# The reciprocal root of the variances on VectorE by Newton steps instead of a square root on ScalarE, in a gated cross-attention and mixture-of-experts kernel

## The chip, the cores and the metric

One core of one Trainium2 chip runs the whole program. The metric is the device time of one execution in microseconds. The kernel before took 3248.48 us, the median of 3 runs (3244.9 to 3255.8).

## The reference

For each of 8 batches of 512 rows of 512 numbers:

```
x  = x + tanh(g0) * attention(layernorm(x), ctx)      # 16 heads of 32, 1601 context rows, q and o quantised to int8 steps
x  = x + tanh(g1) * (experts(h) + shared(h)), h = layernorm(x)
layernorm(x) = (x - mean) / sqrt(var + 1e-5)          # over the 512 numbers of a row
quantise(x): s = max|x| / 127 ; clip(round(x / s), -127, 127) * s
```

The experts part picks 4 of 32 experts for each of the 4096 rows (sigmoid scores, best 2 of 4 groups), each of capacity 128, and a shared gated network runs beside it. The variances of the two layer norms are what the change touches: 4 numbers on each of 128 partitions per batch and norm.

## The kernel before

**Attention part.** The work goes batch by batch (b, 8), in each batch by groups of 4 heads (g, 4), and in each group by 13 tiles of 128 context rows (kt, "key tile"; the last has 65 rows). One step (b, g, kt) is, for each of the 4 heads: a score matmul into one of two PSUM tiles (`scores_of`, L810), its exponential on ScalarE into `probs` (L1038), the matmuls with the values (`heads_of`, L824, one step later), and for 10 of the 13 key tiles (all but 4, 8 and 12) an add of `probs` to `prob_acc` on GpSimd (`add_probs`, L1510; a copy, L1507, for the first tile). The score matmul of a head waits until the exponential two heads earlier has emptied its PSUM tile. `probs` has three buffers in turn.

**Fill work.** Between the score matmuls of a step stand tiles of other work, in an order that is written out by hand (`lead_tiles`, `fill_tiles`) and is the same on TensorE, ScalarE and VectorE: every engine goes through its own instructions in that order, so a wait of one instruction holds all that stand behind it on its engine. For the next group these are the queries, the keys in four pieces (two at kt 0, two at kt 1; ScalarE rounds them, L996, VectorE makes the rest, `k_lo`, L1246), and from kt 3 to 11 the row maxima: 32 pairs of matmuls (L732) into two banks each, read by one VectorE reduction (L1253). There are four such banks, so two pairs can be under way. The keys and queries of a head are stacked by DMAs on SyncE's queue before its first maxima. In group 2 the context tiles of the next batch come in as well (transposes L682, `ctx_hi` on ScalarE L986, `ctx_lo` on VectorE L1218): tiles 0 and 1 at kt 2, tiles 2 and 3 at kt 3, and so on; their DMAs are issued behind those of the keys.

**The two norms.** Their steps stand behind the fill work of a step. For the next batch's x they are in group 2 (`x_part`): at kt 1 the statistics (VectorE, bn_stats and bn_aggr, `variances`), at kt 2 the square root (ScalarE, `deviations`, L929), at kt 3 reciprocal and shift (VectorE, `inverse_std`, L1170 and L1172), at kt 4 and 5 the normalising (ScalarE, L935), then scale, round, clip and integers up to kt 11. For the last batch's h they are in group 1 (`h_part`): statistics at kt 0, square root at kt 1, reciprocal at kt 2, normalising at kt 3 and 4. For batch 0 the x steps stand among the first context tiles, before the attention loop; for the last batch the h steps stand in the experts part, between the first shared tiles, and the rows of the second block are read back from DRAM behind them. Exponential and square root need different tables on ScalarE: a load stands before the first of each (ACT_TABLE_LOAD).

**Experts part.** From about 2530 us: per block of 512 rows the shared network and the routing on VectorE, then the 32 experts with indirect DMAs on GpSimd.

Of the kernel before, what the change touches and what calls it, by code (L numbers as in the profile page):

```python
# [26 lines left out]
P = 128  # L27
# [15 lines left out]
EPS = 1e-5  # L43
ROUND = 12582912.0
CT_SLOTS = 3
SBANKS, NBANKS, HALVES = 2, 4, 3
# [5 lines left out]
CTX_AT = [2, 2, 3, 3, 4, 5, 6, 7, 8, 9, 10, 11, 12]  # L52
X_STATS, X_STD, X_RSTD, X_NORM, X_SCALE, X_ROUND, X_CLIP, X_INT = 1, 2, 3, (4, 5), 6, (7, 8), (8, 9), (10, 11)
O_SCALE, O_ROUND, O_CLIP, O_INT, O_TURN, Y_AT = 3, (4, 5), (5, 6), (7, 8), 9, 10
H_STATS, H_STD, H_RSTD, H_NORM, LATE_HEADS = 0, 1, 2, (3, 4), 10
HALF_TILES = (range(TT // 2), range(TT // 2, TT))
# [180 lines left out]
def build(nc, x, ctx_in, g_xattn, g_ffn, wq, bq, wkv, bkv, wp, bp, gate_w, gate_bias, w1, w2, w3,  # L237
# [15 lines left out]
    with ctx:  # L253
# [12 lines left out]
        lane = sb("lane", [P, E], FP32)  # L266
        eps = sb("eps", [P, 1], FP32)
        rounder = sb("rounder", [P, 2], FP32)
# [21 lines left out]
        mv = sb("mv", [P, TT, 2], FP32)  # L290
        std = sb("std", [P, TT], FP32)
        rstd = sb("rstd", [P, TT], FP32)
# [111 lines left out]
        ctx_raw_in = [sem(f"ctx_raw_in{i}") for i in range(CT_SLOTS)]  # L404
        x_var_ready = sem("x_var_ready")
        x_std_ready = sem("x_std_ready")
        h_var_ready = sem("h_var_ready")
        h_std_ready = sem("h_std_ready")
        x_rstd_ready = sem("x_rstd_ready")
# [500 lines left out]
        def _(act):  # L910
# [14 lines left out]

            def deviations(ready, count, done):

                act.wait_ge(ready, count)
                nc.scalar.activation(std[:, :], mv[:, :, 1], ACT.Sqrt, bias=eps[:, :]).then_inc(done, 1)  # L929

            def normalised(dst, tiles, ready, count, done):
# [19 lines left out]
            def x_part(b, at):  # L951

                if at == X_STD:
                    deviations(x_var_ready, b + 1, x_std_ready)
                for half, tiles in enumerate(HALF_TILES):
                    if at == X_NORM[half]:
                        normalised(xin, tiles, x_rstd_ready, b + 1, x_normed)
                    if at == X_ROUND[half]:
                        rounded(xin, tiles, x_inv_ready, b + 1, x_rounded)
                    if at == X_INT[half]:  # L960
                        integers(xin, tiles, x_clipped, b * TT, x_quantised)
# [9 lines left out]
            def h_part(b, at):  # L971

                if at == H_STD:
                    deviations(h_var_ready, b + 1, h_std_ready)
                for half, tiles in enumerate(HALF_TILES):
                    if at == H_NORM[half]:
                        normalised(work, tiles, h_rstd_ready, b + 1, h_ready)
# [101 lines left out]
            for f in range(B):  # L1079
                for key in ffn_tiles(f):  # L1080
                    tile(key)
                    if key == ("y", B - 1, TT - 1):
                        for at in (H_STD,) + H_NORM:
                            h_part(B - 1, at)
# [15 lines left out]
        def _(dve):  # L1100
# [55 lines left out]

            def variances(ready):
                for t in range(TT):
                    step.mark(V.bn_stats(stats[:, t, :], xin[:, t, :]))
                step.settle()  # L1160
                for t in range(TT):
                    last = V.bn_aggr(mv[:, t, :], stats[:, t, :])
                    if t < TT - 1:
                        step.mark(last)
                last.then_inc(ready, 1)

            def inverse_std(done, n, ready):

                dve.wait_ge(done, n)
                step.mark(V.reciprocal(rstd[:, :], std[:, :]))  # L1170
                step.settle()
                V.scalar_tensor_tensor(out=shift[:, :], in0=mv[:, :, 0], scalar=-1.0, in1=rstd[:, :],  # L1172
                                       op0=ALU.mult, op1=ALU.mult).then_inc(ready, 1)
# [7 lines left out]
            def x_part(b, at):  # L1181

                if at == X_STATS:
                    dve.wait_ge(x_in, (b + 1) * DMA)
                    variances(x_var_ready)
                elif at == X_RSTD:
                    inverse_std(x_std_ready, b + 1, x_rstd_ready)
                elif at == X_SCALE:
                    dve.wait_ge(x_normed, (b + 1) * TT)
                    row_scales(xin, sx)  # L1190
                    dve.sem_inc(x_inv_ready, 1)
                elif at in X_CLIP:
                    clip_rows(xin, HALF_TILES[X_CLIP.index(at)], x_rounded, b * TT, x_clipped)
# [9 lines left out]
            def h_part(b, at):  # L1203

                if at == H_STATS:
                    step.settle()
                    variances(h_var_ready)
                elif at == H_RSTD:
                    inverse_std(h_std_ready, b + 1, h_rstd_ready)

# [260 lines left out]
        def _(pool):  # L1471
            step = Steps(pool, pool_step, pool_wait_carrier)
            G = nc.gpsimd
            for m in (ident, identb):
                step.mark(G.memset(m[:, :], 0.0))
            for m, v in ((onesb, 1.0), (ones, 1.0), (tri, 1.0), (eps, EPS), (zero_rows, 0.0), (slot_init, 0.0)):
                ap = m[:, :, :] if m is slot_init else m[:, :]
# [130 lines left out]
```

## Time and profile before

| | |
|---|---|
| time, median of 3 runs | 3248.48 us (3244.9 to 3255.8) |
| profiled execution | 3254.07 us, span 3251.4 us |
| TensorE matmul busy | 2811.8 us, 86% |
| GpSimd busy | 1806.8 us, 56% |
| VectorE busy | 1727.0 us, 53% |
| ScalarE busy | 1387.3 us, 43% |
| granted TensorE clock, mean | 0.95 |

The span is from the first to the last instruction of the profiled execution, and all times in the rows below count from its start. "Busy" counts instructions that compute. In a row of the timeline a bracket says how long the engine had been idle before the instruction and what ended it. The granted clock is a share of TensorE's full 2.4 GHz; 0.5 is 1.2 GHz.

### The profile page before, as it was taken

Reading aid. Unit: us, or ns where it says so; the run is one execution under the profiler, and the core shown is the slowest. Engines: PE = TensorE matmul, PEld = TensorE weight load, DVE = VectorE, ACT = ScalarE, POOL = GpSimd, SP = SyncE. Lnnn points to the kernel's source line nnn. Section 1 sums busy time; section 2 is a strip of 40 time slices with the busy share of each in tenths; the row PEclk is TensorE's granted clock in tenths of the full one; section 3 lists DMA queues with packets and bytes.
Section 4 is the critical chain, followed back from the end, with each engine's and each line's share of the span. In section 5 each row is a group of like instructions: output and inputs, shape, how many; then the busy total and the mean of one; then the engine's idle time right before and its main releaser. Section 6 shows DMA issues by size and latency. Waiting matters only on the chain. (4 is left out here: it accounts for less than half of the span.)

```text
span 3251.4 us, 42577 instructions
## 1 busy us (share of the span) xinstructions
PE 2811.8 (86%) x14876; PEld 1192.9 (37%) x14876; DVE 1727.0 (53%) x2854; ACT 1387.3 (43%) x2460; POOL 1806.8 (56%) x1570
## 2 busy tenths in 40 slices
PE   5898988899889888988899898889888689996986
PEld 3223333333333333333333333333332344443765
DVE  6566556656565656566556655665653324342222
ACT  3155445644564455455545544564456211010111
POOL 0285566556655665657566656755669223324555
PEclk9799999899999999999999999999999789998999
DMA  4111012110211031103112101211011221222997
GB/s 127 33 44 52 21 34 70 52 35 20 78 48 44 11 97 39 34 21 92 29 34 69 52 21 34 69 52 34 21 51 29 79 89 66 78 78 73 271 279 194
DMA packets 146578, 215.53 MB, mean 66 GB/s; under 512 B 24984, under 2 KB 78232, under 8 KB 146368
## 3 DMA queue, kind: packets, MB, share of 16 engines
q1 hardware_dynamic: 130496, 195.95, 20.0%
q0 software_dynamic: 15872, 16.87, 2.8%
q8 instruction: 120, 1.97, 0.3%
q14 instruction: 90, 0.74, 0.1%
HBM read 126.49 MB, written 34.24 MB: 49 GB/s over the span
## 5 line engine op out<-in xcount | busy, mean ns | idle before, releaser
L1510 POOL TENSOR_TENSOR prob_acc<-prob_acc,probs 128x512 f32<-128x512 f32 x1152 | 1430.1, 1275 | 484.7 <-ACT probs L1038 484.2
L1038 ACT ACTIVATE probs<-s_ps 128x512 f32<-128x512 f32 (+1 forms) x1664 | 939.0, 596 | 806.8 <-PE s_ps L810 787.3
L1253 DVE TENSOR_REDUCE piece_max<-r_all 128x2 f32<-128x802 f32 (+1 forms) x1024 | 965.2, 986 | 229.1 <-PE r_all L732 223.6
L810 PE MATMUL s_ps<-q_stack,k_flat 97*128 97x512 f16 (+1 forms) x1664 | 630.0, 397 | 73.9 <-ACT probs L1038 66.0
L732 PE MATMUL r_all<-k_flat,q_stack 96*128 96x401 f16 (+1 forms) x2048 | 552.3, 353 | 131.7 <-DVE piece_max L1253 80.2
L824 PE MATMUL o_ps<-probs,v_sb 128*32 128x512 f32 (+1 forms) x3328 | 462.8, 629 | 21.4 <-ACT probs L1038 21.4
L810 PEld LDWEIGHTS s_ps<-q_stack,k_flat 97*128 97x128 f16 (+1 forms) x1664 | 161.5, 102 | 635.6 <-ACT probs L1038 411.5
L1507 POOL COPY prob_acc<-probs 128x512 f32<-128x512 f32 x128 | 72.8, 612 | 507.2 <-PE sum_ps L844 372.2
L732 PEld LDWEIGHTS r_all<-k_flat,q_stack 96*128 96x128 f16 x2048 | 178.3, 100 | 392.7 <-DVE piece_max L1253 143.1
L1542 POOL DMA_INDIRECT slot_rows<-payload,slot x128 | 125.3, 979 | 317.7 <-DVE slot L1440 194.7
L1246 DVE SCALAR_TENSOR_TENSOR k_lo<-r_all,bk_col,k_hi 128x400 f16<-128x400 f32 (+1 forms) x128 | 81.8, 639 | 280.7 <-ACT k_hi L996 280.7
L779 PE MATMUL r_all<-probs,k_flat 128*128 128x512 f32 x512 | 225.9, 603 | 2.0 <-DMA k_flat<-in_L_ffn_shared_down 2.0
L1225 DVE TENSOR_TENSOR v_sb<-r_all,bv_row 128x512 f32<-128x512 f32 (+1 forms) x104 | 71.8, 691 | 195.3 <-PE r_all L692 195.2
L996 ACT ACTIVATE k_hi<-r_all,bk_col 128x400 f16<-128x400 f32 (+1 forms) x128 | 76.5, 598 | 197.5 <-PE r_all L721 197.5
L1568 POOL DMA_INDIRECT out_rows<-probs,slot_init x64 | 99.7, 1559 | 96.1 <-DMA out_rows<-probs,slot_init 50.0
L779 PEld LDWEIGHTS r_all<-probs,k_flat 128*128 128x128 f32 x512 | 98.5, 194 | 123.1 <-issue 121.0
L692 PE MATMUL r_all<-wkv_hi,ctx_hi 128*128 128x512 f16 (+1 forms) x416 | 113.1, 396 | 21.0 <-DVE piece_max L1253 18.5
L824 PEld LDWEIGHTS o_ps<-probs,v_sb 128*32 128x32 f32 (+1 forms) x3328 | 66.7, 109 | 159.6 <-issue 88.0
L797 PE MATMUL r_all<-k_flat,probs 128*128 128x512 f32 x256 | 119.6, 628 | 0.9 <-DVE probs L1396 0.9
L1218 DVE TENSOR_TENSOR ctx_lo<-r_all,ctx_hi 128x512 f16<-128x512 f32 (+1 forms) x104 | 69.2, 673 | 76.0 <-ACT ctx_hi L986 75.6
L721 PE MATMUL r_all<-ctx_hi,wkv_hi 128*128 128x400 f16 (+1 forms) x512 | 109.4, 336 | 0.0
L721 PE MATMUL r_all<-ctx_lo,wkv_hi 128*128 128x400 f16 (+1 forms) x512 | 109.1, 336 | 0.0
(193 smaller groups left out, 2752.8 us busy)
## 6 DMA issues: line engine op xcount, KB each, us to landing
k_flat<-k_hi SPq DMA_DIRECT2D x256, 100.1 KB, 2.2
ctx_raw<-in_ctx SPq DMA_DIRECT2D x96, 256.0 KB, 2.9
v_sb<-in_L_ffn_w SPq DMA_DIRECT2D x48, 512.0 KB
xin<-in_x SPq DMA_DIRECT2D x16, 1024.0 KB, 5.6
k_flat<-k_lo SPq DMA_DIRECT2D x128, 100.1 KB, 2.2
ctx_hi<-in_L_ffn_w SPq DMA_DIRECT2D x24, 512.0 KB
ctx_lo<-in_L_ffn_w SPq DMA_DIRECT2D x24, 512.0 KB
q_stack<-q_hi SPq DMA_DIRECT2D x256, 32.0 KB, 1.8
```

The lines of the kernel that those rows point to most:

```text
L692: last = nc.tensor.matmul(ps[0:w, :], a[:, c, t * P:t * P + w], wt[:, 1, c, :], start=(n == 0), stop=(n == 3 * DC - 1))
L721: last = nc.tensor.matmul(ps[:, 0:w], wt[:, 0, c, g * P:(g + 1) * P], a[:, c, at:at + w], start=(n == 0), stop=(n == 3 * DC - 1))
L732: last = nc.tensor.matmul(ps[:, 0:w], q_stack[0:KSPLIT, g % 2, j, qt * P:(qt + 1) * P], k_stack[0:KSPLIT, g % 2, j, at:at + w], start=True ...
L779: last = nc.tensor.matmul(ps[:, :], wt[:, c, f * P:(f + 1) * P], hT[:, c, :], start=(c == 0), stop=(c == DC - 1))
L797: last = nc.tensor.matmul(ps[:, :], actT[:, f, t * P:(t + 1) * P], sd[:, f, :], start=(f == 0), stop=(f == FSC - 1))
L810: nc.tensor.matmul(s_ps[j % SBANKS][0:w, :], k_stack[:, g % 2, j, kt * P:kt * P + w], q_stack[:, g % 2, j, :], start=True, stop=True).then ...
L824: last = nc.tensor.matmul(o_ps[j * DH:(j + 1) * DH, :], v_sb[0:w, kt, h * DH:(h + 1) * DH], probs[0:w, slot, j, :], start=(kt == 0), stop= ...
L1038: nc.scalar.activation(probs[0:w, slot, j, :], s_ps[j % SBANKS][0:w, :], ACT.Exp).then_inc(probs_ready, 1)
L1253: V.reduce_max(piece_max[:, j * TT + qt, 2 * i:2 * i + 2], r_all[:, k:k + 2, 0:MAX_WIDE[i]], X_AXIS).then_inc(free_of(*key), 1)
L1510: last = G.tensor_tensor(prob_acc[:, j, :], prob_acc[:, j, :], probs[:, slot, j, :], ALU.add)
L1542: G.indirect_dma_start(out=slot_scr, out_offset=bass.IndirectOffsetOnAxis(ap=slot[:, t, k:k + 1], axis=0), in_=payload[:, t, k, :], in_off ...
L1568: G.indirect_dma_start(out=out, out_offset=bass.IndirectOffsetOnAxis(ap=e_slots[:, e, 0:1].bitcast(I32), axis=0), in_=e_y[e % 2][:, h * HA ...
```

## The change

The square root on ScalarE and its semaphores go. VectorE now makes 1 / sqrt(var + eps) by itself: it adds eps, takes a first guess from the bits of the number (a shift to the right, times -1, plus a constant), and betters it by three Newton steps of three instructions each, every one waiting for the one before. All later steps of x and h move one key tile forward, since one step of the sequence is gone.

```
-X_STATS, X_STD, X_RSTD, X_NORM, X_SCALE, X_ROUND, X_CLIP, X_INT = 1, 2, 3, (4, 5), 6, (7, 8), (8, 9), (10, 11)
+X_STATS, X_RSTD, X_NORM, X_SCALE, X_ROUND, X_CLIP, X_INT = 1, 2, (3, 4), 5, (6, 7), (7, 8), (9, 10)
-H_STATS, H_STD, H_RSTD, H_NORM, LATE_HEADS = 0, 1, 2, (3, 4), 10
+H_STATS, H_RSTD, H_NORM, LATE_HEADS = 0, 1, (2, 3), 10
...
-            def deviations(ready, count, done):
-                act.wait_ge(ready, count)
-                nc.scalar.activation(std[:, :], mv[:, :, 1], ACT.Sqrt, bias=eps[:, :]).then_inc(done, 1)
...
-            def inverse_std(done, n, ready):
-                dve.wait_ge(done, n)
-                step.mark(V.reciprocal(rstd[:, :], std[:, :]))
-                step.settle()
+            def inverse_std(ready):
+                step.mark(V.tensor_scalar(var[:, :], mv[:, :, 1], EPS, None, ALU.add))
+                step.settle()
+                step.mark(V.tensor_scalar(shift[:, :].bitcast(I32), var[:, :].bitcast(I32), 1, None, ALU.logical_shift_right))
+                step.settle()
+                step.mark(V.tensor_scalar(rstd[:, :].bitcast(I32), shift[:, :].bitcast(I32), -1.0, RSQRT_SEED, ALU.mult, ALU.add))
+                step.settle()
+                for _ in range(NEWTON):
+                    step.mark(V.scalar_tensor_tensor(out=shift[:, :], in0=rstd[:, :], scalar=-0.5, in1=rstd[:, :],
+                                                     op0=ALU.mult, op1=ALU.mult))
+                    step.settle()
+                    step.mark(V.tensor_tensor(shift[:, :], shift[:, :], var[:, :], ALU.mult))
+                    step.settle()
+                    step.mark(V.scalar_tensor_tensor(out=rstd[:, :], in0=shift[:, :], scalar=1.5, in1=rstd[:, :],
+                                                     op0=ALU.add, op1=ALU.mult))
+                    step.settle()
                 V.scalar_tensor_tensor(out=shift[:, :], in0=mv[:, :, 0], scalar=-1.0, in1=rstd[:, :],
                                        op0=ALU.mult, op1=ALU.mult).then_inc(ready, 1)
```

`NEWTON` is 3. `variances` now ends with a wait for its own last bn_aggr, in place of a signal to ScalarE, and the memset of the constant `eps` on GpSimd is gone.

## Rows read from the trace of the kernel before

**Rows 1.** Groups of instructions on ScalarE: busy us, mean ns, idle before.

```profile
L929 ACT ACT_TABLE_LOAD x16 | 20.5, 1283 | 0.3
L1038 ACT ACT_TABLE_LOAD x15 | 19.2, 1283 | 0.3
```

**Rows 2.** Timeline at an h site (batch 1, group 1): start, duration, instruction.

```profile
512.18 4.95 POOL L1510 TENSOR_TENSOR prob_acc<-prob_acc,probs 128x512 f32<-128x512 f32 x4
...
516.51 1.28 ACT L929 ACT_TABLE_LOAD   x1
516.53 0.64 DVE L1246 SCALAR_TENSOR_TENSOR k_lo<-r_all,bk_col,k_hi 128x400 f16<-128x400 f32 x1 [2.93 <-ACT k_hi L996]
...
519.42 3.32 ACT L1038 ACTIVATE probs<-s_ps 128x512 f32<-128x512 f32 x6
520.07 0.88 PE L810 MATMUL s_ps<-q_stack,k_flat 97*128 97x512 f16 x2 [2.78 <-ACT probs L1038]
...
521.86 0.67 PE L732 MATMUL r_all<-k_flat,q_stack 96*128 96x401 f16 x2
...
524.33 0.61 PE L810 MATMUL s_ps<-q_stack,k_flat 97*128 97x512 f16 x1
```

**Rows 3.** Timeline at the same place of batch 0, where no statistics stand.

```profile
203.61 12.29 POOL L1510 TENSOR_TENSOR prob_acc<-prob_acc,probs 128x512 f32<-128x512 f32 x10
...
207.96 0.64 DVE L1246 SCALAR_TENSOR_TENSOR k_lo<-r_all,bk_col,k_hi 128x400 f16<-128x400 f32 x1 [2.93 <-ACT k_hi L996]
...
212.05 0.85 PE L732 MATMUL r_all<-k_flat,q_stack 96*128 96x401 f16 x2 [1.44 <-DMA k_flat<-k_hi]
```

**Rows 4.** Timeline of dependent small VectorE instructions, with no GpSimd add beside them.

```profile
2583.01 0.17 DVE L1375 TENSOR_SCALAR wsum<-wsum 128x4 f32<-128x4 f32 x1
2583.21 0.18 DVE L1377 RECIPROCAL wrec<-wsum 128x4 f32<-128x4 f32 x1
```

**Rows 5.** Durations ns (min/median/max) of two lines, and timelines where VectorE meets GpSimd.

```profile
L1108 DVE TENSOR_SCALAR so<-amax x8: 169/1306/1322, 444.1 to 2539.7; 128x4 f32<-128x4 f32 x8
...
444.07 1.30 DVE L1108 TENSOR_SCALAR so<-amax 128x4 f32<-128x4 f32 x1
444.09 3.70 POOL L1517 TENSOR_TENSOR xin<-xin,bp_row 128x512 f32<-128x512 f32 x3
...
L1510 POOL TENSOR_TENSOR prob_acc<-prob_acc,probs x1152: 1250/1267/1732, 141.1 to 2530.2; 128x512 f32<-128x512 f32 x192
...
491.34 0.69 DVE L1268 TENSOR_TENSOR xin<-xin,work 128x512 f32<-128x512 f32 x1
491.43 1.73 POOL L1510 TENSOR_TENSOR prob_acc<-prob_acc,probs 128x512 f32<-128x512 f32 x1 [1.75 <-ACT probs L1038]
```

**Rows 6.** Timeline at an x site (batch 0, group 2).

```profile
267.25 8.63 POOL L1510 TENSOR_TENSOR prob_acc<-prob_acc,probs 128x512 f32<-128x512 f32 x7
...
274.80 1.28 ACT L929 ACT_TABLE_LOAD   x1
...
275.30 0.38 PE L810 MATMUL s_ps<-q_stack,k_flat 97*128 97x512 f16 x1
...
276.10 1.88 DVE L1253 TENSOR_REDUCE piece_max<-r_all 128x2 f32<-128x802 f32 x2
...
281.58 0.66 PE L682 MATMUL r_all<-ident,ctx_raw 128*128 128x128 f32 x4 [1.84 <-DMA ctx_raw<-in_ctx]
```

**Rows 7.** Timeline at the first exponentials.

```profile
138.58 0.88 PE L810 MATMUL s_ps<-q_stack,k_flat 97*128 97x512 f16 x2 [2.17 <-ACT probs L1038]
```

**Rows 8.** Timeline at the last h, in the experts part.

```profile
2593.46 0.30 ACT L929 ACTIVATE std<-mv,eps 128x4 f32<-128x4 f32 x1 [8.71 <-DVE mv L1162]
...
2594.20 2.93 ACT L935 ACTIVATE work<-xin,shift,rstd 128x512 f32<-128x512 f32 x4 [0.44 <-DVE shift L1172]
...
2608.09 3.38 PE L766 MATMUL r_all<-ident,probs 128*128 128x128 f32 x16 [20.43 <-DMA probs<-h_rows]
```

**Rows 9.** Busy time by stretch: us, each engine's, granted clock, DMA share, GB/s.

```profile
522.30:525.60 3.30, 3.30 (x13) 0.77 (x13) 0.99 (x1) 1.00 (x2) 3.30 (x4) 0.52 0.69 162
```

More of the change, by code:

```diff
@@ L44 @@
 ROUND = 12582912.0
+RSQRT_SEED, NEWTON = 1597463007.0, 3
 CT_SLOTS = 3
@@ L266, in build @@
         lane = sb("lane", [P, E], FP32)
-        eps = sb("eps", [P, 1], FP32)
         rounder = sb("rounder", [P, 2], FP32)
@@ L290, in build @@
         mv = sb("mv", [P, TT, 2], FP32)
-        std = sb("std", [P, TT], FP32)
+        var = sb("var", [P, TT], FP32)
         rstd = sb("rstd", [P, TT], FP32)
@@ L404, in build @@
         ctx_raw_in = [sem(f"ctx_raw_in{i}") for i in range(CT_SLOTS)]
[L405 to L408, printed above, removed]
         x_rstd_ready = sem("x_rstd_ready")
@@ L951, in x_part @@
             def x_part(b, at):
-                if at == X_STD:
-                    deviations(x_var_ready, b + 1, x_std_ready)
                 for half, tiles in enumerate(HALF_TILES):
@@ L971, in h_part @@
             def h_part(b, at):
-                if at == H_STD:
-                    deviations(h_var_ready, b + 1, h_std_ready)
                 for half, tiles in enumerate(HALF_TILES):
@@ L1082, in _ @@
                     if key == ("y", B - 1, TT - 1):
-                        for at in (H_STD,) + H_NORM:
+                        for at in H_NORM:
                             h_part(B - 1, at)
@@ L1155, in _, with variances @@
             V.tensor_scalar(bp_row[:, :], bp_row[:, :], tanhs[:, 0:1], None, ALU.mult).then_inc(row_consts_ready, 1)
-            def variances(ready):
+            def variances():
                 for t in range(TT):
@@ L1161, in variances @@
                 for t in range(TT):
[L1162 to L1165, printed above, removed]
-            def inverse_std(done, n, ready):
-                dve.wait_ge(done, n)
-                step.mark(V.reciprocal(rstd[:, :], std[:, :]))
-                step.settle()
+                    step.mark(V.bn_aggr(mv[:, t, :], stats[:, t, :]))
+                step.settle()
+            def inverse_std(ready):
[14 more added lines that the diff above has]
+                    step.settle()
                 V.scalar_tensor_tensor(out=shift[:, :], in0=mv[:, :, 0], scalar=-1.0, in1=rstd[:, :],
@@ L1184, in x_part @@
                     dve.wait_ge(x_in, (b + 1) * DMA)
-                    variances(x_var_ready)
+                    variances()
                 elif at == X_RSTD:
-                    inverse_std(x_std_ready, b + 1, x_rstd_ready)
+                    inverse_std(x_rstd_ready)
                 elif at == X_SCALE:
@@ L1206, in h_part @@
                     step.settle()
-                    variances(h_var_ready)
+                    variances()
                 elif at == H_RSTD:
-                    inverse_std(h_std_ready, b + 1, h_rstd_ready)
+                    inverse_std(h_rstd_ready)
             def tile(key):
@@ L1475, in _ @@
                 step.mark(G.memset(m[:, :], 0.0))
-            for m, v in ((onesb, 1.0), (ones, 1.0), (tri, 1.0), (eps, EPS), (zero_rows, 0.0), (slot_init, 0.0)):
+            for m, v in ((onesb, 1.0), (ones, 1.0), (tri, 1.0), (zero_rows, 0.0), (slot_init, 0.0)):
                 ap = m[:, :, :] if m is slot_init else m[:, :]
```

## The prediction, made before the change was run

> **What bounds the kernel now.** I read the page's engine shares first: TensorE is busy 86% of the span, GpSimd 56%, VectorE 53%, ScalarE 43%. In the attention part (about 137 to 2530 us) nothing but TensorE is near full, so a change on another engine moves the time only where TensorE waits for that engine. Next the groups of ScalarE's instructions: 16 table loads at the square root and 15 at the first exponential behind it, 1.28 us each [rows 1]. Apart from the first statistics and the last, they come in 14 pairs: 7 with the statistics of h (group 1 of a batch, "h sites") and 7 with those of the next x (group 2, "x sites"). Then I read the timeline at one site of each kind; the sites of a kind repeat within a few tenths.
>
> At an h site the reader is to see ScalarE's exponentials of key tile 2 start only at 519.42, behind the loads that begin at 516.51, and TensorE idle 2.78 us for them [rows 2]. The same place exists once without statistics, in batch 0: there the first pair of maxima starts 212.05 - 208.60 = 3.45 us after the last k_lo, and what it waits for is the DMA of the stacked keys; at the h site it is 521.86 - 517.17 = 4.69 us [rows 2, 3]. So the stall is 2.78 us long but only 1.24 us of it count: the DMA is next behind it.
>
> **What is removed.** Per pair two loads and a 0.30 us square root, 2.9 us of ScalarE. At an h site this is worth the 1.24 us above, 7 times: -8.7. At an x site TensorE's next fixed point is the arrival of a context tile at 281.58, for which it idles 1.84 us already [rows 6]; so there nothing. 
>
> **What is added.** VectorE had two small instructions (reciprocal, shift); now it has 13, each waiting for the one before: add, bit shift, multiply-add, three times three of Newton, shift. Such instructions follow each other every 0.20 to 0.21 us when nothing disturbs them [rows 4]: 12 x 0.205 + 0.16 = 2.6 us, against 0.4. That is the cost alone, and it would be covered: VectorE is idle 4 us at the h site.
>
> But GpSimd adds probabilities in these places, and the trace shows that it and VectorE exclude each other. The 4-element tensor_scalar at L1108 takes 0.17 us alone, and 1.3 when a GpSimd add is under way: 444.07 + 1.30 = 445.37 is the end of the first of the adds begun at 444.09, 3.70 / 3 = 1.23 us each [rows 5]. The other way round, an add begun 0.1 us after a VectorE tensor_tensor with both operands in SBUF took 1.73 instead of 1.27 us, at all 7 places of this kind [rows 5]. Not shown is a small two-operand instruction that meets an add in progress; by the symmetry I take it to wait for the add's end, like L1108. Of the 13, three are tensor_scalars and ten have two SBUF operands, so all 13 can wait. When one gets through at the end of an add, the next add has begun before its successor arrives: one add (1.24 us from start to start) per instruction, as long as GpSimd has adds.
>
> The Trainium skill ("SBUF — State Buffer", Who interferes with whom) says the same for both forms: two SBUF inputs on VectorE contend with a GpSimd instruction that reads SBUF, and whoever is second is blocked for the whole instruction. It is the reason why I hold the undisturbed chain unlikely.
>
> *h site.* The chain starts at 517.2, behind the last k_lo. With ScalarE free, the four exponentials of key tile 2 run 516.5 to 518.9, and GpSimd goes on without a gap from 517.13; the undisturbed site of batch 0 shows it adding straight through this window [rows 3]. Adds end at 518.4, 519.6, 520.8 and 522.1: four instructions wait. Then GpSimd is out of work, because the change has also moved the first half of the normalising from key tile 3 to 2: ScalarE stands before it, waiting for the chain, and the exponentials of key tile 3 are queued behind. So the other nine take 9 x 0.205: chain ready at 524.0. Two normalisings of 2.93 / 4 = 0.73 [rows 8]: 525.4. Exponential 0.6: 526.0. The third score matmul of key tile 3 needs it, and started at 524.33 before: +1.7 us. Bounds: -1.24 (no waits; then chain 519.8, normalised 521.3, exponential 521.9, hidden by the DMA and the matmuls behind it), and +1.7, since more than four waits are not possible for the reason given; a longer stretch at half clock is rival C. 7 x 1.7 = +11.9.
>
> *x site.* VectorE reached the first two maxima at 276.10 [rows 6]; now the chain stands before them. GpSimd ended key tile 2's adds at 275.88, and ScalarE, now free at 274.8, gives it the next two at 275.4 and 276.3 (0.6 us behind 274.8, and behind the score matmul of 275.30): adds end at 277.1 and 278.4. Instructions 1 and 2 wait for these, 3 to 5 slip in, 6 waits for the third add (278.9 to 280.1). The fourth can't come: its score matmul is queued on TensorE behind the third pair of maxima, which needs a bank that VectorE has not read. Seven more: 281.65. Two reductions of 0.94: the third pair of maxima starts at 282.6, the transposes of context tiles 2 and 3 at 283.5 and 284.1. The latter started at 281.58: +2.5 us. Bounds: undisturbed, the chain ends at 278.8 and the same count gives 281.4, just inside the DMA's cover: 0. 7 x 2.5 = +17.9 (unrounded 2.55). Both delays hit TensorE and VectorE alike, and TensorE is nearly full in what follows, so I let them stand.
>
> *First x:* GpSimd has no adds there; VectorE has slack in the context tiles; 0 to +0.5, taken 0. *Last h:* it is on the chain that ends last: VectorE's aggregate to the normalising took 2594.20 - 2593.46 = 0.74 us, now 2.6; TensorE waits 20 us for the rows that follow [rows 8]. No adds run: +1.9. The sigmoid's second load, which also goes, is off the chain. The other steps moved one key tile earlier (scale, round, clip, integers) keep their neighbours: 0, within 0.5 a site. The constant's memset: 0.
>
> **Sum**, against the profiled execution (span 3251.4, its time 3254.1): -1.3 + 11.9 + 17.9 + 1.9 = +30.4, so 3284.5. The profiled one is 5.6 above the median 3248.5 of the three runs shown (3244.9 to 3255.8); the same difference on the median gives 3278.9, rounded 3279.
>
> **Rivals.**
> A. Only the three tensor_scalars wait. For it: L1108 shows no more than that. h site: three waits (520.8), then ten: 522.9, third score at 525.0, +0.6. x site: two waits, then free: 280.65, context tile 3 at 283.15, +1.6. Sum -1.3 + 4.5 + 11 + 1.9 = +16.1: 3265 on the median. Much the same comes out (3261) if all wait but the x sites' delay is made good in later slack.
> B. The other side: small instructions find gaps between the adds, nothing waits. -1.3 - 8.7 + 0 + 1.9 = -8.1: 3240, faster but under the bound. It decides at whether the chain is ready by 520 at the h site and 279 at the x site. Against it: L1108 (so) has a median of 1306 ns over 8 [rows 5].
> C. The clock: after the h site's idle time the granted clock was 0.52 for 3.3 us, 1.2 instead of 2.4 GHz [rows 9]. TensorE would now idle 522.2 to 526.0 at each h site. One more such stretch costs 3.3 / 2 = 1.65 us, 7 times: +11.6 on top: 3291.
> D. The change doesn't do what it says: a load stays before the first exponential since the tanh's is another. The rest is as forecast: 3280.
>
> **How the numbers follow.** Forecast 0.50, A 0.19 (both forms), B 0.14, C 0.12, D 0.05. Below 0.3%, 9.7 us, a measurement of this kernel can't tell. Forecast, A, C and D are slower by more, though a smaller share of A and of the forecast may fall under: slower 0.77. B lies under the bound but reaches over it if the half-clock stretches vanish with the idle time (7 x 1.65): faster 0.10, same 0.13. The range leaves out most of B and little of C: 3249 to 3294.
>
> **What would show it.** No table load between the first exponential and the last of the attention part. The lines of Newton with means well over 0.17 us, 0.5 to 1 us at h and x sites, and adds that end where they end. The last k_lo to the first maxima at h sites 3.45; the third score behind it about 9 us after k_lo (now 7.2). At x sites the context tile's idle time gone, and the first reduction at about 281.7. If the chain's instructions all take 0.16 to 0.18 us beside running adds, B is right and I am wrong; if only the first three are long, A.

## The result, and the profile after

The changed kernel takes 3308.1 us in the median of 4 runs (3305.1 to 3311.3), beside 3246.7 for the kernel before (4 runs, 3239.1 to 3255.8). The ratio is 1.019, 95% interval 1.0165 to 1.0215. It is slower, as forecast, but by 61 us and not by 30, and above the forecast's range (3249 to 3294). The profiled execution has a span of 3306.6 us, 55.2 more than before.

A row of the page's costliest groups (line, engine, operation, count | busy us, mean ns | idle before, releaser):

```profile
L728 PE MATMUL r_all<-k_flat,q_stack 96*128 96x401 f16 (+1 forms) x2048 | 567.6, 361 | 177.0 <-DVE piece_max L1250 117.5
```

The groups of ScalarE's table loads that are left:

```profile
L909 ACT ACT_TABLE_LOAD x1 | 1.3, 1283 | 1.1 <-DVE rounder L1120 1.1
L1006 ACT ACT_TABLE_LOAD x1 | 1.3, 1283 | 0.0
```

So the change does what it says: the 31 loads of [rows 1] are gone and two are left in the whole program, at the tanh and at the first sigmoid, so the exponentials use the tanh's table. Part of what TensorE lost shows in the first row: the maxima's matmuls now wait 117.5 us for VectorE to read their banks, and they waited 80 before.

To see where the 55 us are I cut the attention part at the row maxima, one per group of heads. VectorE's timeline has 31 such groups. The three row maxima around groups 1 and 2 of batch 1, in the kernel before:

```profile
495.66 0.22 DVE L1257 TENSOR_REDUCE row_max<-piece_max 128x16 f32<-128x64 f32 x1
561.15 0.22 DVE L1257 TENSOR_REDUCE row_max<-piece_max 128x16 f32<-128x64 f32 x1
641.87 0.22 DVE L1257 TENSOR_REDUCE row_max<-piece_max 128x16 f32<-128x64 f32 x1
```

and after:

```profile
499.13 0.22 DVE L1254 TENSOR_REDUCE row_max<-piece_max 128x16 f32<-128x64 f32 x1
567.65 0.22 DVE L1254 TENSOR_REDUCE row_max<-piece_max 128x16 f32<-128x64 f32 x1
651.76 0.22 DVE L1254 TENSOR_REDUCE row_max<-piece_max 128x16 f32<-128x64 f32 x1
```

Group 1 went from 65.49 to 68.52 us here, group 2 from 80.72 to 84.11. Over all batches (means of 7, from such rows):

| | before | after | difference, times 7 |
|---|---|---|---|
| group 1 (h site), batches 1 to 7 | 65.42 | 68.49 | +21.5 |
| group 2 (x site), batches 0 to 6 | 78.68 | 83.86 | +36.3 |
| group 3, batches 0 to 6 | 80.62 | 80.26 | -2.5 |

The rest: the first row maximum comes 2.2 later, batch 0's first group is 2.4 shorter, the other seven first groups together 1.0 shorter, the last batch's group 2 is 1.45 longer, batch 0's group 1 0.1, and all behind the last row maximum is 0.25 shorter. The sum is 55.2.

The timeline at the h site of batch 1, which answers to [rows 2]:

```profile
515.65 9.87 POOL L1507 TENSOR_TENSOR prob_acc<-prob_acc,probs 128x512 f32<-128x512 f32 x8
...
520.00 0.64 DVE L1243 SCALAR_TENSOR_TENSOR k_lo<-r_all,bk_col,k_hi 128x400 f16<-128x400 f32 x1 [2.86 <-ACT k_hi L983]
520.55 1.32 DVE L1154 TENSOR_SCALAR var<-mv 128x4 f32<-128x4 f32 x1
521.91 1.19 DVE L1156 TENSOR_SCALAR shift<-var 128x4 int32<-128x4 int32 x1
...
524.35 1.19 DVE L1161 SCALAR_TENSOR_TENSOR shift<-rstd 128x4 f32<-128x4 f32 x1
525.58 0.16 DVE L1164 TENSOR_TENSOR shift<-shift,var 128x4 f32<-128x4 f32 x1
...
527.15 0.16 DVE L1169 SCALAR_TENSOR_TENSOR shift<-mv,rstd 128x4 f32<-128x4 f32 x1
...
524.11 0.52 PE L728 MATMUL r_all<-k_flat,q_stack 96*128 96x401 f16 x2 [1.46 <-DMA k_flat<-k_hi]
...
529.40 0.61 PE L806 MATMUL s_ps<-q_stack,k_flat 97*128 97x512 f16 x1 [3.78 <-ACT probs L1025]
```

Four of the 13 instructions last as long as an add of GpSimd; when its adds end, at 525.52, the others take 0.16 us. The third score starts 529.40 - 520.64 = 8.76 us behind the last k_lo, where I had said about 9 (the working gives 8.8) and before it was 7.16.

The x site of batch 1, which answers to [rows 6], and in the same group, 20 us later, the scale of x:

```profile
592.26 0.91 DVE L1154 TENSOR_SCALAR var<-mv 128x4 f32<-128x4 f32 x1
...
595.23 1.14 DVE L1161 SCALAR_TENSOR_TENSOR shift<-rstd 128x4 f32<-128x4 f32 x1
...
597.38 0.16 DVE L1169 SCALAR_TENSOR_TENSOR shift<-mv,rstd 128x4 f32<-128x4 f32 x1
...
598.50 0.85 PE L728 MATMUL r_all<-k_flat,q_stack 96*128 96x401 f16 x2 [4.19 <-DVE piece_max L1250]
...
599.58 1.91 PE L678 MATMUL r_all<-ident,ctx_raw 128*128 128x128 f32 x8
...
610.00 8.64 POOL L1507 TENSOR_TENSOR prob_acc<-prob_acc,probs 128x512 f32<-128x512 f32 x7 [8.18 <-ACT probs L1025]
...
615.37 0.86 DVE L1095 TENSOR_SCALAR sx<-amax 128x4 f32<-128x4 f32 x1
617.63 0.82 PE L728 MATMUL r_all<-k_flat,q_stack 96*128 96x401 f16 x2 [2.41 <-DVE piece_max L1250]
```

The chain has nearly the pattern of the forecast: two wait, four slip in (forecast three), the next waits, six run free. It ends 10.5 us behind the last k_lo (10.6 forecast). But the scale, moved to key tile 5, meets adds at every x site (0.86 us), where before it met them at two of the seven (0.18 at the others), and TensorE stops for VectorE there, 2.41 us. That stop isn't new: in the kernel before it is 2.01 us at five x sites and 2.7 at two, batch 1 among them, so the change makes it 0.2 us longer in the mean. Behind both stops the matmuls are slow again (0.85 and 0.82 for a pair of maxima that takes 0.51 elsewhere). The transposes of context tile 3 (in the changed kernel the second four of the eight from 599.58) and the stop at the scale, in the kernel before:

```profile
592.05 0.66 PE L682 MATMUL r_all<-ident,ctx_raw 128*128 128x128 f32 x4 [1.62 <-DMA ctx_raw<-in_ctx]
...
617.26 0.50 PE L732 MATMUL r_all<-k_flat,q_stack 96*128 96x401 f16 x2 [2.69 <-DVE piece_max L1253]
```

### The profile page after: what moved, and what is told of

Read it like the earlier page. It is cut to its first block and busy times, and to the rows that moved or that the text cites. A ratio compares the mean times of both kernels' runs of the same rounds, so it can differ in the third digit from the quotient of the medians.

```text
span 3306.6 us, 42672 instructions
## 1 busy us (share of the span) xinstructions
PE 2825.5 (85%) x14836; PEld 1192.1 (36%) x14876; DVE 1820.6 (55%) x3030; ACT 1342.7 (41%) x2412; POOL 1809.4 (55%) x1569
## 5 line engine op out<-in xcount | busy, mean ns | idle before, releaser
L728 PE MATMUL r_all<-k_flat,q_stack 96*128 96x401 f16 (+1 forms) x2048 | 567.6, 361 | 177.0 <-DVE piece_max L1250 117.5
L717 PE MATMUL r_all<-ctx_hi,wkv_lo 128*128 128x400 f16 (+1 forms) x512 | 108.4, 334 | 0.0
```

The costliest lines, as they stand in the source:

```text
L717: last = nc.tensor.matmul(ps[:, 0:w], wt[:, 0, c, g * P:(g + 1) * P], a[:, c, at:at + w], start=(n == 0), stop=(n == 3 * DC - 1))
L728: last = nc.tensor.matmul(ps[:, 0:w], q_stack[0:KSPLIT, g % 2, j, qt * P:(qt + 1) * P], k_stack[0:KSPLIT, g % 2, j, at:at + w], start=True ...
```

## The experiments

Two theories of the excess stood at the start: the waits on GpSimd's adds plus the clock (P, C), or the moved steps (M). The rivals were that the number of instructions costs by itself (N), and that the chain alone made all of it. Each time stands beside the kernel before on the same chip. It is that of a single execution, but for pool_timed (median of 12) and pool_moved (median of 4), with 17 of the kernel before. The groups are means of 7 in the one profiled execution.

| kernel | us | before beside it | group 1 | group 2 | group 3 |
|---|---|---|---|---|---|
| newton0 | 3282.3 | 3240.7 | 66.43 | 82.18 | 80.48 |
| norm_back | 3303.7 | 3240.7 | 70.38 | 80.67 | 81.86 |
| after_tiny_adds | 3182.6 | 3240.7 | 64.65 | 74.59 | 79.39 |
| before_tiny_adds | 3228.0 | 3240.7 | 66.28 | 76.42 | 82.38 |
| filler | 3295.3 | 3254.5 | 66.74 | 82.94 | 80.28 |
| late | 3347.5 | 3254.5 | 72.26 | 85.21 | 81.25 |
| pool_chain | 3239.9 | 3254.5 | 63.67 | 78.59 | 80.70 |
| pool_timed (the kernel of pool_chain) | 3235.6 | 3243.6 | 63.39 | 79.18 | 80.99 |
| pool_moved | 3259.3 | 3243.6 | 63.77 | 82.12 | 80.09 |

The two profiles of the same kernel differ by 0.9 us in groups 2 and 3 together (159.3 and 160.2): smaller differences between single profiles say little.

### newton0: the chain without its Newton steps

```diff
-RSQRT_SEED, NEWTON = 1597463007.0, 3
+RSQRT_SEED, NEWTON = 1597463007.0, 0
```

> The Newton steps are left out (the root stays the guess from the bits, so its value is not the reference's): the chain has 4 instructions instead of 13, all else as in the changed kernel. In the changed kernel a batch's group 1 (from one row maximum to the next) is 68.5 us and group 2 83.9, before 65.4 and 78.7. Theory P (small dependent VectorE instructions each wait for a GpSimd add in progress): at an h site the 4 instructions that waited are still there and still take 1.19 to 1.32 us; only the nine of 0.2 go. Chain end 1.8 us earlier, third score of key tile 3 7.0 us behind the last k_lo instead of 8.76. At an x site two wait, two are short: the chain ends 2.7 us earlier. Group 1 66.7, group 2 81.2, the kernel 31 us shorter than the changed one: about 3277. If the half-clock stretch behind the h stall goes with the shorter stall, group 1 is 65.3 and the kernel 3267. Rival N (the number of instructions alone, no waiting): the chain is 0.8 us long and the sites are those of before: 3250. Rival M (the steps moved one key tile earlier are what costs): no change, 3306.

Its h site in batch 1:

```profile
517.54 0.64 DVE L1243 SCALAR_TENSOR_TENSOR k_lo<-r_all,bk_col,k_hi 128x400 f16<-128x400 f32 x1 [2.86 <-ACT k_hi L983]
...
521.87 1.18 DVE L1169 SCALAR_TENSOR_TENSOR shift<-mv,rstd 128x4 f32<-128x4 f32 x1
...
525.14 0.61 PE L806 MATMUL s_ps<-q_stack,k_flat 97*128 97x512 f16 x1 [0.76 <-ACT probs L1025]
```

The last of the four, 0.16 us in the changed kernel, now takes 1.18, since it is fourth. The third score is 6.96 us behind k_lo (7.0 expected), group 1 66.4 (66.7), the kernel 3282 (3277). It is still 42 us over the kernel before beside it, with nine of the thirteen instructions gone: rival N, which had 3250, falls. Group 2 fell by 1.7, not 2.7. Group 1 is still 1.0 above that of before although its third score comes 0.2 earlier, so the lateness of the chain isn't all of it. The granted clock over group 1 is 0.92 to 0.95 here and 0.97 in the kernel before, batches 1 to 7.

### norm_back: only the moved steps undone

```diff
-X_STATS, X_RSTD, X_NORM, X_SCALE, X_ROUND, X_CLIP, X_INT = 1, 2, (3, 4), 5, (6, 7), (7, 8), (9, 10)
+X_STATS, X_RSTD, X_NORM, X_SCALE, X_ROUND, X_CLIP, X_INT = 1, 2, (4, 5), 6, (7, 8), (8, 9), (10, 11)
-H_STATS, H_RSTD, H_NORM, LATE_HEADS = 0, 1, (2, 3), 10
+H_STATS, H_RSTD, H_NORM, LATE_HEADS = 0, 1, (3, 4), 10
```

> Only the moved steps go back to the key tiles of before (x: normalising 4 and 5, scale 6, rounding 7 and 8, clipping 8 and 9, integers 10 and 11; h: normalising 3 and 4); the chains stay on VectorE at key tiles 2 and 1. Theory P: at an h site ScalarE is no longer held before key tile 3, so GpSimd gets key tile 3's adds too and more than 4 of the 13 wait, up to 8: the chain ends up to 4 us later, but TensorE has the scores meanwhile; group 1 between 67.5 and 71. At an x site the chain is as before it (2 or 3 waits), the scale and clipping fall where they fell before, means back from 1055 to about 730 ns for the clipping: group 2 81 to 82 instead of 83.9, if my forecast term for the chain (2.5 us) was right. Rival M: both groups back to 65.4 and 78.7. Rival K (the chain's delay alone, through the clock, made all of the +5.2): group 2 stays at 83.5 to 84.

The h site in batch 1:

```profile
517.83 13.50 POOL L1507 TENSOR_TENSOR prob_acc<-prob_acc,probs 128x512 f32<-128x512 f32 x11
...
521.50 1.30 DVE L1154 TENSOR_SCALAR var<-mv 128x4 f32<-128x4 f32 x1
...
530.17 1.18 DVE L1164 TENSOR_TENSOR shift<-shift,var 128x4 f32<-128x4 f32 x1
531.39 0.16 DVE L1166 SCALAR_TENSOR_TENSOR rstd<-shift,rstd 128x4 f32<-128x4 f32 x1
...
533.30 0.85 PE L728 MATMUL r_all<-k_flat,q_stack 96*128 96x401 f16 x2 [5.83 <-DVE piece_max L1250]
```

From 521.50 to 531.35 there are eight instructions of 1.18 to 1.30, one add each; the ninth is free because GpSimd's adds ended at 531.33. ScalarE, no longer held, had fed GpSimd four adds more, and so four more waited. That is the plainest proof of the rule by which the chain was priced, and group 1 is 1.9 us worse for it. At the x sites the clipping is back from 1055 to 727 ns, group 2 is 3.2 us shorter than in the changed kernel (80.7, just under the 81 to 82 expected), group 3 1.6 longer, at a granted clock of 0.96 over the group against 0.98. Rival M (both groups back to before) and rival K (group 2 unmoved) both fall. Groups 2 and 3 together are 159.3 before, 162.5 here, 164.1 in the changed kernel. By these sums the chain costs 3.2 a batch and the moved steps 1.6 on top, which the forecast had at 0; the difference in group 3 blurs this, and a cleaner split stands under pool_moved.

### after_tiny_adds and before_tiny_adds: the adds cut short in both

```diff
-                        last = G.tensor_tensor(prob_acc[:, j, :], prob_acc[:, j, :], probs[:, slot, j, :], ALU.add)
+                        last = G.tensor_tensor(prob_acc[:, j, 0:8], prob_acc[:, j, 0:8], probs[:, slot, j, 0:8], ALU.add)
```

> The changed kernel, but every GpSimd addition of probabilities adds only 8 of 512 columns (most of that sum is left out): same instructions and waits, without their time. Theory P: the chain's instructions are 0.16 to 0.2 us throughout and follow each other every 0.20; the chain is 2.6 us. Compared with the kernel before with the same cut: group 1 shorter by 1.2 us, group 2 the same within 0.5, start 1.3 shorter, so 5 to 11 us less in all. Rival N (13 serial instructions cost what they cost, adds or not) and rival M (moved steps): the changed one stays 40 to 60 us longer than the other.

> The kernel before with the same cut of the GpSimd additions to 8 of 512 columns. It is the partner of the run above. Theory P: the statistics instructions and two-operand instructions that met adds get shorter, TensorE's share hardly moves: 0 to 15 us shorter than 3251, and 5 to 11 us longer than its partner. Rivals N and M: 40 to 60 us shorter than its partner.

Groups of the changed kernel with the cut:

```profile
L1507 POOL TENSOR_TENSOR prob_acc<-prob_acc,probs 128x8 f32<-128x8 f32 x1152 | 233.8, 204 | 1540.9 <-ACT probs L1025 1540.7
...
L1154 DVE TENSOR_SCALAR var<-mv 128x4 f32<-128x4 f32 x16 | 2.8, 178 | 0.0
L1161 DVE SCALAR_TENSOR_TENSOR shift<-rstd 128x4 f32<-128x4 f32 x48 | 7.8, 163 | 1.6
L1176 DVE TENSOR_SCALAR xin<-xin 128x512 f32<-128x512 f32 x32 | 12.0, 418 | 0.0
```

With the adds short, the chain's instructions are 0.16 to 0.18 us (995 ns was L1154's mean in the changed kernel), and the change is no longer slower by 60 us but faster by 45. The whole loss therefore depends on GpSimd's adds. Rivals N and M, which had it 40 to 60 slower here, fall. Group 1 gains 1.6 (1.2 expected). But I had expected 5 to 11 in all: groups 2 and 3 gain 1.8 and 3.0 a batch, where I had said 0. Which of the two freed things (ScalarE's 2.9 us, the earlier steps) gives that stays open; some of it is clock, since over the seven groups 3 the mean granted clock is 0.99 with the change and 0.96 without.

### filler: the idle time filled with matmuls

```diff
+            def filler(s, count):
+                pe.wait_ge(sums_copied, s // KT)
+                for _ in range(count):
+                    nc.tensor.matmul(sum_ps[:, :], identb[:, :], wqT[:, 0, :], start=True, stop=True)
...
                     scores_of(s, g, j)
+                    if (g, kt, j) == (2, 3, SBANKS) and b + 1 < B:
+                        filler(s, 14)
...
                     if j == SBANKS - 1 and kt:
                         heads_of(s - 1)
+                    if (g, kt, j) == (1, 3, SBANKS - 1) and b:
+                        filler(s, 14)
```

> The changed kernel with 14 matmuls more (128x128 by 128x512 bf16, about 0.21 us each at full clock, 3 us) at each site, into sums that are overwritten afterwards: at an h site behind the first maxima, where TensorE idles 3.8 us for ScalarE; at an x site ahead of the third pair of maxima, where it idles 4.2 us for VectorE. They lie inside the idle time, so they delay nothing. Theory C (part of the cost is the half clock behind the idle time): the maxima and scores behind the stall take 0.4 and 0.25 us again instead of 0.85 and 0.63, group 1 falls from 68.5 by the 1.35 us that my sum did not have, to 67.1; group 2 from 83.9 by 1 to 3. Rival (the stall alone and what is queued behind it; the clock costs nothing since VectorE sets the pace there): both groups within 0.3 of 68.5 and 83.9. A second rival: filler work lengthens them (up to +0.5) since it runs into what follows.

Its h site in batch 1, and two stretches behind the stall of that place, first of the changed kernel, then of this one (in columns: each engine's busy us, granted clock, DMA share, GB/s):

```profile
529.31 2.97 PE L839 MATMUL sum_ps<-wqT,identb 128*128 128x512 bf16 x13 [0.16 <-issue]
...
532.90 0.39 PE L806 MATMUL s_ps<-q_stack,k_flat 97*128 97x512 f16 x1 [0.63 <-ACT probs L1034]
```

```profile
529.30:533.90 4.60, 4.50 (x14) 1.59 (x14) 2.97 (x3) 3.83 (x8) 4.48 (x4) 0.50 0.00 1
```

```profile
532.90:537.10 4.20, 3.74 (x21) 1.18 (x22) 3.42 (x4) 3.97 (x7) 4.17 (x4) 1.00 0.05 17
```

Nothing of the wait is taken away: the third score starts 8.74 us behind the last k_lo, as in the changed kernel (8.76). But TensorE was busy in between, and the granted clock behind it is 1.00 (2.4 GHz) where it was 0.50 (1.2 GHz): a score takes 0.39 us instead of 0.61. Group 1 falls from 68.49 to 66.74 in the mean (66.3 in the median).

That is not yet the clock's share of the 3.07 us, since the kernel before has half-clock time of its own behind its h stall [rows 9], and the filler takes all of it away: the granted clock over group 1 is 0.97 before, 0.93 in the changed kernel (0.95 in batch 1) and 1.00 in five of the filler's seven sites. Group 1 cut at the last k_lo and at the third score, means of batches 1 to 7 (filler: of those five), us:

| | to the end of the last k_lo | to the third score | to the row maximum |
|---|---|---|---|
| before | 21.50 | 7.11 | 36.82 |
| after | 21.50 | 8.76 | 38.22 |
| filler | 21.51 | 8.75 | 36.06 |

So of the 3.07 us the late score is 1.65, 11.6 over seven, and what comes behind it 1.40, 9.8 over seven. The work behind is the same, takes 36.1 at full clock, and has lost 2.2 to the half clock in the changed kernel where it had lost 0.8 before. At the other two sites (batches 3 and 4) the half clock came earlier and the added matmuls ran in it, 4.4 and 4.6 us instead of 3.0; the third score came 0.8 and 2.2 us later there. As a remedy the filler is not sure.

At the x sites the clock is 1.00 behind the first stop too, but group 2 falls by 0.9 only: there VectorE is the busier of the two behind the stop (4.36 of 4.80 us, TensorE 3.92). The second stop was not filled.

### late: the chains at key tile 4

```diff
+X_STATS, X_RSTD, X_NORM, X_SCALE, X_ROUND, X_CLIP, X_INT = 1, 4, (5, 6), 7, (8, 9), (9, 10), (10, 11)
+H_STATS, H_RSTD, H_NORM, LATE_HEADS = 0, 4, (5, 6), 10
```

> The changed kernel with both chains put at key tile 4 and the normalising at 5 and 6 (x: scale 7, rounding 8 and 9, clipping 9 and 10, integers 10 and 11). The chain then stands in the row of maxima and not before them, and key tile 4 is one that GpSimd does not add. Theory P: the stalls before the first maxima go (group 1: last k_lo to first maxima 3.47, no 3.8 us idle); what waits there are depends on adds of key tile 3 still under way: 0 to 4 of 13 wait. Group 1 64.5 to 66.5, group 2 78 to 81, the kernel 3235 to 3270. Rival M (what costs is the order of the moved steps, or the length of the chain wherever it is): group 1 68 or more, group 2 83 or more, 3300.

The h site in batch 1:

```profile
535.20 4.94 POOL L1507 TENSOR_TENSOR prob_acc<-prob_acc,probs 128x512 f32<-128x512 f32 x4 [2.50 <-ACT probs L1025]
...
538.98 1.18 DVE L1161 SCALAR_TENSOR_TENSOR shift<-rstd 128x4 f32<-128x4 f32 x1
...
542.88 0.85 PE L728 MATMUL r_all<-k_flat,q_stack 96*128 96x400 f16 x2 [5.69 <-DVE piece_max L1250]
```

A miss: the slowest of all, 3347.5 where I had 3235 to 3270, with both groups longer than in the changed kernel (72.3 and 85.2). Four instructions wait, as bounded, but what I expected of the place was wrong. At key tile 2 part of the chain lies under a DMA that TensorE waits for anyway; in the row of maxima nothing lies under it, since TensorE gets two pairs of maxima ahead and then stops for 5.69 us. The chain costs least where TensorE waits for something else, and where GpSimd is idle in the queue's plan is no measure of where it is idle in time.

### pool_chain: the chain on GpSimd

The steps stand at before's key tiles (as in norm_back). VectorE makes the statistics only; GpSimd's queue gets:

```diff
+            def inverse_std(which, n, ready):
+                pool.wait_ge(which, n)
+                step.mark(G.tensor_scalar(var[:, :], mv[:, :, 1], EPS, None, ALU.add))
+                step.settle()
+                step.mark(G.tensor_scalar(rstd[:, :].bitcast(I32), var[:, :].bitcast(I32), -0.5, RSQRT_SEED, ALU.mult, ALU.add))
...
             for b, g, kt in steps():
+                if g == 1 and b and kt == 1:
+                    inverse_std(h_var_ready, b, h_rstd_ready)
+                if g == 2 and b + 1 < B and kt == 3:
+                    inverse_std(x_var_ready, b + 2, x_rstd_ready)
                 if kt in POOL_STEPS:
```

> The statistics stay on VectorE, but the chain runs on GpSimd, in its queue between the adds of key tiles 0 and 1 (h) and 2 and 3 (x), so that none of its instructions can meet an add; the shift is made by a multiplication by -0.5 of the integer, and a Newton step is four instructions: 16 in all, of 0.1 to 0.25 us. Normalising, scale, rounding, clipping and integers are at the key tiles of before. Theory P: TensorE and VectorE never wait for it; GpSimd's adds come 3 to 5 us later. At h sites last k_lo to first maxima 3.47 as with DMA, group 1 64.2 (1.2 under before); group 2 77 to 79; the start 1.3 shorter: 3225 to 3245. Rival S: GpSimd's delay comes back through the slots of probabilities (an exponential waits for the add three key tiles before): group 1 up to 67, group 2 up to 81, 3250 to 3265. Rival N (the chain's length on any engine): as the changed kernel, 3300.

> The kernel of the run pool_chain again, timed. In one look it was 14.6 us under the kernel before (3239.9 to 3254.5). Its groups sum to 14.8 us less (last row maximum 2462.0 against 2476.9, first 1.6 later): group 1 shorter by 1.75 each, nothing in group 2. So a ratio of 0.9955 to 0.9975 if that holds; the rival, that the one look was luck of the clock's stretches (they differ by up to 2 us between the same groups of one run), gives 1.000 within 0.0015.

GpSimd's and VectorE's rows at the h site of batch 1 in the timed kernel's profile:

```profile
512.93 0.23 POOL L1493 TENSOR_SCALAR var<-mv 128x4 f32<-128x4 f32 x1
513.24 0.19 POOL L1495 TENSOR_SCALAR rstd<-var 128x4 int32<-128x4 int32 x1
...
517.15 0.23 POOL L1508 TENSOR_SCALAR shift<-shift 128x4 f32<-128x4 f32 x1
517.15 0.64 DVE L1223 SCALAR_TENSOR_TENSOR k_lo<-r_all,bk_col,k_hi 128x400 f16<-128x400 f32 x1 [2.93 <-ACT k_hi L985]
517.34 4.94 POOL L1487 TENSOR_TENSOR prob_acc<-prob_acc,probs 128x512 f32<-128x512 f32 x4
```

The 16 instructions take 4.45 us, in order with the adds, and end during the last k_lo. Group 1 is 63.7 and 63.4 in the two profiles (65.4 before), group 2 78.6 and 79.2 (78.7). Timed, the median is 3235.6 (12 runs) against 3243.6 (17), ratio 0.9973, interval 0.9959 to 0.9987: it beats both kernels, the one before by 8 to 9 us, as expected (0.9955 to 0.9975). That is less than the 0.3% that I took as the bound; single executions of the two kernels overlap, and only the many together tell them apart. Rival S is small at the h sites: the adds begin 4.5 us later, and one exponential of key tile 3 waits 0.50 us for an add.

### pool_moved: the same, with the steps where the change has them

```diff
+X_STATS, X_RSTD, X_NORM, X_SCALE, X_ROUND, X_CLIP, X_INT = 1, 2, (3, 4), 5, (6, 7), (7, 8), (9, 10)
+H_STATS, H_RSTD, H_NORM, LATE_HEADS = 0, 1, (2, 3), 10
```

> As pool_chain, but normalising, scale, rounding, clipping and integers one key tile earlier, as the change has them. It shows the moved steps without the chain on VectorE. In pool_chain group 1 is 63.7, groups 2 and 3 together 159.3; in the changed kernel 68.5 and 164.1, with the moved steps undone there 162.5. Theory P with moved steps as a cost of their own (clipping of the rounded rows meets GpSimd's adds, 1055 instead of 727 ns, just ahead of the maxima): groups 2 and 3 together 160.5 to 162, group 1 the same, the kernel 5 to 15 us longer than pool_chain. Rival (the moved steps cost nothing by themselves; in the changed kernel they only met the late chain): within 3 us of pool_chain. Against both: with the additions cut, the moved order was 4.8 us a batch shorter in these two groups, so it could also be shorter here by up to 3 a batch.

Its groups of clipping and scale:

```profile
L1160 DVE TENSOR_SCALAR xin<-xin 128x512 f32<-128x512 f32 x32 | 30.1, 982 | 0.0
...
L1097 DVE TENSOR_SCALAR sx<-amax 128x4 f32<-128x4 f32 x8 | 6.1, 768 | 0.3
```

Ratio to before 1.0044 (1.0030 to 1.0059), 3259.3 us. Group 1 is that of pool_chain (63.8 to 63.7), so the earlier normalising of h costs nothing by itself. Groups 2 and 3 together are 162.2, against 159.3 and 160.2 in the two profiles with the steps at before's key tiles: the moved steps of x cost 2.0 to 2.9 us a batch with no chain on VectorE. In time the kernel is 23.7 us longer than pool_timed (3259.3 against 3235.6), where I had 5 to 15: the direction is right, the size a miss. Clipping takes 982 ns and not 726, the scale 768 (351 before).

Where the chain costs and where the moved steps do comes out when group 2 is cut at the transposes of context tile 3, for which the chain is a term of the forecast; scale and clipping lie behind them. Means of batches 0 to 6, us:

| | to the end of the last k_lo | to the transposes of tile 3 | to the row maximum |
|---|---|---|---|
| before | 19.38 | 11.04 | 48.26 |
| after | 19.38 | 13.21 | 51.28 |
| norm_back (chain, steps not moved) | 19.37 | 13.44 | 47.86 |
| pool_timed (neither) | 19.62 | 10.92 | 48.64 |
| pool_moved (steps moved, no chain) | 19.38 | 10.96 | 51.78 |

The chain on VectorE makes the middle column 2.2 to 2.4 us longer and leaves the last alone; the moved steps make the last 3.0 to 3.5 longer and leave the middle alone. With the adds cut short the moved order is no loss there (44.52 against 46.21), so it is the adds that the moved steps meet. Four clippings of an x take 4.6 us in the changed kernel and 3.1 before; how the 3.0 divide over clipping, scale and clock behind them isn't shown.

## Why the prediction was right and wrong

*Direction and mechanism: right.* The small dependent instructions each wait for one GpSimd add (newton0, norm_back with its eight, both tiny kernels). The Trainium skill ("SBUF — State Buffer", Who interferes with whom) says that VectorE with two SBUF inputs is shut out by a GpSimd instruction that reads SBUF, for that whole instruction; the runs agree, 1.1 to 1.2 us against 0.16 for L1161. Rivals A and B fall with this, for the fourth instruction, the first with two operands, waited like the others. D falls: a tanh's table serves the exponentials.

*h site, +1.7 forecast, +3.07 measured (+11.9 against +21.5).* The chain and the third score came within 0.1 us of the working. What failed is the sentence "a longer stretch at half clock is rival C", which set the clock at nothing in the forecast and gave it 0.12. The late score itself is worth 1.65, the term of the sum; behind it the changed kernel takes 1.40 longer a site (38.22 us against 36.82) for work that takes 36.1 at full clock, near the 1.65 that rival C had. So C was the right case at the h sites, and the idle time that feeds it (3.8 us forecast, 3.78 measured) stood in the text.

*x site, +2.55 forecast, +5.18 measured, less 0.36 in group 3 (+17.9 against +33.8).* The step that failed is "The other steps moved one key tile earlier (scale, round, clip, integers) keep their neighbours: 0, within 0.5 a site". They meet adds that they did not meet before, and the part of group 2 in which they lie is 3.0 longer, 21.1 us over seven; with the steps put back it isn't (norm_back), and with the chain gone and the steps moved it is (pool_moved). The chain's own part was 2.2, near the 2.55 that I had. Of the two together the filler gives 0.9 to the clock behind the first stop.

*The ends.* The places of [rows 7, 8], after:

```profile
139.98 0.88 PE L806 MATMUL s_ps<-q_stack,k_flat 97*128 97x512 f16 x2 [0.74 <-ACT probs L1025]
...
2647.61 0.38 DVE L1149 BATCH_NORM_AGGREGATE mv<-stats 128x2 f32<-128x6 f32 x4
...
2650.60 2.93 ACT L926 ACTIVATE work<-xin,shift,rstd 128x512 f32<-128x512 f32 x4 [12.58 <-DVE shift L1169]
...
2664.54 3.67 PE L762 MATMUL r_all<-ident,probs 128*128 128x128 f32 x16 [22.32 <-DMA probs<-h_rows]
```

TensorE's wait for the first exponential fell from 2.17 to 0.74 us, about as said. But the zero for the first x was wrong: the first row maximum comes at 130.60 instead of 128.40, and in newton0 at 128.55, so the Newton steps seem to be on the path there. With the 2.4 gained in the next group that makes -0.2 instead of -1.3. Last h: from the aggregate's end to the normalising 2.6 us, as said, and the rows' transposes are 1.0 us later, counted from the last row maximum; but all behind that maximum is 0.25 shorter in the end, not 1.9 longer. Where the 1.0 comes back isn't shown; the mean granted clock behind the last row maximum is 0.92, and 0.91 before. The last batch's group 2, with no site in it, is 1.45 longer, a term that I didn't have. It goes with the clock: a stretch at half clock lies in it that the kernel before doesn't have there. That group before, and after (columns as above):

```profile
2418.39:2476.88 58.49, 53.70 (x321) 18.99 (x317) 36.16 (x46) 32.75 (x60) 45.00 (x40) 1.00 0.12 29
```

```profile
2472.39:2532.33 59.94, 54.98 (x320) 19.07 (x317) 36.14 (x46) 32.84 (x60) 45.08 (x40) 0.97 0.12 28
```

*Where the range failed:* 3294 was its upper end, made of forecast and C. The measured 3308 is C at the h sites plus the moved steps at the x sites. Both were in the text, one as a rival alone and the other as a zero; the range took in either, but not the two together.

## What to carry to other kernels

Before putting a chain of small dependent instructions on VectorE, look at what GpSimd does in that place: each of them can cost one whole GpSimd instruction, so price the chain by the adds under way and not by its length, or give it to GpSimd's own queue. A schedule shifted "by one step" is an edit of its own: look up every instruction that it moves against the other engines. And where a stall is lengthened, count the clock behind it as part of the stall.

## What the hardware showed that I had not expected

- Filling idle time with work that is thrown away made the kernel shorter, in the one execution that there is: a span of 3293.5 instead of 3306.6 us with 14 matmuls more a site, and a granted clock of 0.951 instead of 0.939 over the span.
- The larger single-input instructions depend on the adds too: clipping (128x512, tensor_scalar) took 418 ns with short adds, 727 in the kernel before and 1055 where it was moved under more of them.
- A group without a site takes one of two lengths, the last batch's group 2 58.5 us in eight of eleven profiles and 59.8 to 60.1 in three. The granted clock over the group is 1.00 in all of the eight and 0.97 in all of the three, which have a stretch at half clock in it. So such a stretch costs 1.3 to 1.6 us there, and whether it comes differs between kernels that do the same work in this group.
- GpSimd makes the guess out of the bits by a multiplication of the integer view by -0.5 and an addition, 0.19 us, and dependent instructions of 128x4 follow each other there every 0.28 us, against 0.20 on VectorE.
